# Setup of a gated cross-attention decoder: TensorE turns while the first transfer is under way, step sizes by halves, two activation tables loaded early

## What is computed

```python
x = x + tanh(g_xattn[0]) * selective_scan(ctx, layernorm(x), ...)      # this case's stretch
x = x + tanh(g_ffn[0])   * mixture_of_experts(layernorm(x), ...)       # 64 experts, 8 chosen, 64 slots each
x = x + tanh(g_xattn[1]) * attention(layernorm(x), ctx, ...)           # 16 heads, 8 key/value heads
x = x + tanh(g_ffn[1])   * ternary_weight_ffn(layernorm(x), ...)
```

```python
x  = einsum('bld,ed->bel', hidden_states, in_proj_w)            # 256 inner channels
x  = silu(causal_conv(x, conv_w, 4 taps) + conv_b)              # "u" below
dt_low, Bm, Cm = split(einsum('bdl,ed->bel', x, x_proj_w), [8, 24], axis=1)
dt = softplus(einsum('brl,dr->bdl', dt_low, dt_proj_w) + dt_proj_b)   # the step sizes
# for each token: state = state * exp(dt * A) + (dt * u) * B;  y = sum_n state * C, n = 0..15
y  = (y + D * x) * silu(z)
```

## Time and profile before

| | |
|---|---|
| Median of 3 runs | 565.86 us (564.44 to 566.52) |
| Profiled execution, own time | 564.71 us |
| its span in the trace | 563.0 us |
| TensorE busy | 483.5 us (86%) |
| VectorE busy | 456.3 us (81%) |
| ScalarE busy | 371.2 us (66%) |
| GpSimd busy | 283.3 us (50%) |
| bytes moved by DMA | 61.65 MB, 109 GB/s in the mean |

### The profile page before, as it was taken

The page is one execution under the profiler, slowest core; times in us unless marked ns, Lnnn a source line. Parts: engine busy times, 40 slices in busy tenths (PEclk is TensorE's granted clock), DMA queues, the critical chain, the costliest instruction groups (busy, mean ns, idle before and its releaser), DMA issues.

```text
span 563.0 us, 10640 instructions
## 1 busy us (share of the span) xinstructions
PE 483.5 (86%) x3374; PEld 396.7 (70%) x3374; DVE 456.3 (81%) x1213; ACT 371.2 (66%) x863; POOL 283.3 (50%) x254
## 2 busy tenths in 40 slices
PE   5955877778899799999899999989699898998835
PEld 3443555555689667767798999978699788996714
DVE  2879999999985678887568757987889879776887
ACT  2785766667346465878575766689466896788644
POOL 1118999989211755610586388434884343233111
PEclk9956999989999899999899999999999999999876
DMA  5976993322177799872421023200433000000000
GB/s 152 237 208 208 322 300 135 109 98 81 50 217 240 247 308 264 263 196 80 165 66 39 2 58 64 33 0 2 66 61 45 2 2 1 19 3 1 1 19 19
DMA packets 52477, 61.65 MB, mean 109 GB/s; under 512 B 6204, under 2 KB 42662, under 8 KB 52422
## 3 DMA queue, kind: packets, MB, share of 16 engines
q1 hardware_dynamic: 48582, 49.43, 30.1%
q0 software_dynamic: 3840, 11.54, 9.2%
HBM read 54.27 MB, written 6.69 MB: 108 GB/s over the span
## 4 chain that ended last, share of the span: by engine, by line
PE 37%; DVE 22%; issue 21%; POOL 9%; ACT 6%; DMA 3%; DVEq 0%; POOLq 0%; SPq 0%; ACTq 0%
PE ps L1661 6%; DVE hst L1913 5%; PE ps L1600 4%; PE ps L1601 4%; PE ps L1602 4%; PE ps L1650 3%; DVE hc L1925 3%; PE ps L1518 3%; POOL dbu L628 3%; POOL pn L711 2%; POOL G L695 2%; DMA ebuf<-state_rows 2%; PE ps L1554 2%; PE ps L1539 2%; POOL G L673 1%
## 5 line engine op out<-in xcount | busy, mean ns | idle before, releaser
L711 POOL TENSOR_TENSOR pn<-pr,pinv 128x512 f32<-128x512 f32 x64 | 67.6, 1058 | 88.2 <-DVE pinv L2326 87.8
L628 POOL TENSOR_TENSOR dbu<-du,brow 128x512 f32<-128x512 f32 x64 | 92.9, 1481 | 25.4 <-DVE du L1903 22.1
L1913 DVE TENSOR_TENSOR_SCAN hst<-ps,dbu 128x512 f32<-128x512 f32 x64 | 74.6, 1202 | 0.2 <-POOL dbu L628 0.2
L1057 ACT ACTIVATE pr<-ebuf,smin 128x256 f32<-128x256 f32 x128 | 63.8, 502 | 13.4 <-POOL pn L711 6.7
L854 ACT ACTIVATE ps<-dtv,amat 128x510 f32<-128x510 f32 x64 | 44.4, 694 | 36.0 <-DVE hst L1913 33.1
L1661 PE MATMUL ps<-pT,cS 128*128 128x256 f32 x256 | 66.5, 382 | 0.0
L673 POOL DMA_INDIRECT G<-token_rows,idx_x x32 | 37.8, 1180 | 43.3 <-DVE wkv L2050 20.8
L695 POOL DMA_INDIRECT G<-expert_out,idx_g x48 | 51.4, 1070 | 11.6 <-issue 10.5
L1600 PE MATMUL ps<-xnT,mqk 128*128 128x256 f32 x128 | 46.9, 366 | 6.7 <-DVE qT L2287 3.5
L2317 DVE CUSTOM_DVE_ANT_0 ebuf<-ps,mbias 128x256 f32<-128x256 f32 x128 | 49.0, 420 | 4.2 <-issue 3.9
L1302 PE MATMUL ps<-hc,ident 128*128 128x512 f32 x68 | 37.1, 636 | 16.1 <-DVE hc L1925 15.9
(11 more groups left out here) (381 smaller groups left out, 1438.3 us busy)
## 6 DMA issues: line engine op xcount, KB each, us to landing
brow<-state_rows SPq DMA_DIRECT2D x16, 512.0 KB, 5.0
wdn<-in_L_ffn_wd SPq DMA_DIRECT2D x12, 384.0 KB, 8.3
ebuf<-state_rows SPq DMA_DIRECT2D x17, 256.0 KB, 3.8
wgu<-in_L_ffn_wg SPq DMA_DIRECT2D x11, 384.0 KB, 6.0
wgu<-in_L_ffn_wu SPq DMA_DIRECT2D x11, 384.0 KB, 8.7
expert_out<-xn SPq DMA_DIRECT2D x11, 256.0 KB, 5.3
wq<-in_L_xattn_Wq SPq DMA_DIRECT2D x2, 1024.0 KB, 7.4
wo<-in_L_xattn_Wo SPq DMA_DIRECT2D x1, 2048.0 KB, 11.6
```

The source lines that it names most:

```text
L628: nc.gpsimd.tensor_tensor(dbu[:, j, :], du[:, j % 2, at:at + 512], brow[:, pair % BRING, j // 2, :], ALU.mult).then_inc(pool_dbu, 1)
L711: nc.gpsimd.tensor_tensor(pn[:, h % 2], pr[:, h % 2], pinv[:, h % 2, :].unsqueeze(2).to_broadcast([P, 2, L]), ALU.mult)\
L1057: last = A(pr[:, h % 2, tt, :], sneg[:, h % 2, tt, :], ACT.Exp, scale=-1.0, bias=smin[:, h % 2, tt:tt + 1], accum_out=psum_[:, h % 2, tt:t ...
L1913: V.tensor_tensor_scan(hst[:, j, :], bank(j % 2), dbu[:, j, :], 0.0, ALU.mult, ALU.add)\
```

## The change

1. TensorE, once the identity is there and before it waits for the context, turns the identity 16 times into bank 7. Nobody reads the result.
2. ScalarE applies Silu to a spare value after its first copies, and Exp to a spare value after the last Relu, so that the tables for these functions are loaded there.
3. Raw step sizes and all operations on them go by half: first tiles 0 and 1 of tokens 0 to 511, then of tokens 512 to 1023. Each operation has 512 columns instead of 1024, and there are twice as many. TensorE's loop over L1288 has the half outside and the tile inside. VectorE still makes both halves ahead of the first scan; the two small memsets of decay columns come between the halves.
4. Waits follow: GpSimd waits for du of half 0 at pair 0 and of half 1 at pair 8, ScalarE for all four dt at scan 32, SyncE before Wk and Wv for all four dt.

```diff
@@ SyncE
-            sp_.wait_ge(dt_ready, 2)
+            sp_.wait_ge(dt_ready, 4)
@@ GpSimd, drive(pair, j)
-                if pair == 0 and j < 2:
-                    pool.wait_ge(du_ready, j + 1)
+                if pair % (NS // 2) == 0 and j < 2:
+                    pool.wait_ge(du_ready, 4 * pair // NS + j + 1)
@@ ScalarE
             A(winT[:, 0], bank(5).rearrange("p (k e) -> p k e", k=NCONV), ACT.Copy).then_inc(winT_ready, 1)
+            act.wait_ge(consts_ready, 3)
+            chain.link(A(spare_table[:, 0:1], mhalf[:, 0:1], ACT.Silu))
...
-            for d in range(DT):
-                act.wait_ge(dtraw_done, 2 * d + 2)
-                chain.link(A(sp[2 * d][:], ps[:, 2 * d:2 * d + 2, :].rearrange("p a b -> p (a b)"), ACT.Abs,
-                             bias=dtb[:, d:d + 1]))
-                A(sp[2 * d + 1][:], sp[2 * d][:], ACT.Exp, scale=-1.0).then_inc(sp_exp, 1)
-            for d in range(DT):
-                act.wait_ge(sp_u, d + 1)
-                A(dtv[:, d], sp[2 * d][:], ACT.Ln).then_inc(sp_ln, 1)
-                A((rest, dtlow)[d][:], ps[:, 2 * d:2 * d + 2, :].rearrange("p a b -> p (a b)"), ACT.Relu,
-                  bias=dtb[:, d:d + 1]).then_inc(sp_relu, 1)
+            def at(hb):
+                return slice(512 * hb, 512 * hb + 512)
+
+            for hb in range(2):
+                for d in range(DT):
+                    act.wait_ge(dtraw_done, 2 * hb + d + 1)
+                    chain.link(A(sp[2 * d][:, at(hb)], bank(2 * d + hb), ACT.Abs, bias=dtb[:, d:d + 1]))
+                    A(sp[2 * d + 1][:, at(hb)], sp[2 * d][:, at(hb)], ACT.Exp, scale=-1.0).then_inc(sp_exp, 1)
+            for hb in range(2):
+                for d in range(DT):
+                    act.wait_ge(sp_u, 2 * hb + d + 1)
+                    A(dtv[:, d, at(hb)], sp[2 * d][:, at(hb)], ACT.Ln).then_inc(sp_ln, 1)
+                for d in range(DT):
+                    A((rest, dtlow)[d][:, at(hb)], bank(2 * d + hb), ACT.Relu, bias=dtb[:, d:d + 1]).then_inc(sp_relu, 1)
+            A(spare_table[:, 1:2], mhalf[:, 0:1], ACT.Exp)
...
+                if i == 32:
+                    act.wait_ge(dt_ready, 4)
@@ TensorE
+            def keep_busy(k, count):
+                for _ in range(count):
+                    pe.transpose(ps[:, k, 0:P], ident[:], ident[:])
+
             pe.wait_ge(consts_ready, 1)
+            keep_busy(7, 16)
             pe.wait_ge(d_ctx, 16)
...
-            for d in range(DT):
-                for hb in range(2):
-                    pe.wait_ge(dtlow_ready, hb + 1)
+            for hb in range(2):
+                pe.wait_ge(dtlow_ready, hb + 1)
+                for d in range(DT):
                     pe.matmul(bank(2 * d + hb), dtwT[32:32 + DTR, P * d:P * d + P],
@@ VectorE
-            for d in range(DT):
-                dve.wait_ge(sp_exp, d + 1)
-                V.tensor_scalar(sp[2 * d][:], sp[2 * d + 1][:], 1.0, None, ALU.add).then_inc(sp_u, 1)
...
-                V.tensor_tensor(du[:, d], dtv[:, d], u[:, d], ALU.mult).then_inc(du_ready, 1)
+            for hb in range(2):
+                for d in range(DT):
+                    dve.wait_ge(sp_exp, 2 * hb + d + 1)
+                    V.tensor_scalar(sp[2 * d][:, at(hb)], sp[2 * d + 1][:, at(hb)], 1.0, None, ALU.add).then_inc(sp_u, 1)
+                for d in range(DT):
+                    dve.wait_ge(sp_u, 2 * hb + d + 1)
+                    chain.step(V.scalar_tensor_tensor(sp[2 * d + 1][:, at(hb)], sp[2 * d][:, at(hb)], -1.0,
+                                                      sp[2 * d + 1][:, at(hb)], ALU.add, ALU.subtract))
+
+            def step_sizes(hb, d):
+                n = 2 * hb + d + 1
+                dve.wait_ge(sp_ln, n)
+                chain.link(V.tensor_tensor(dtv[:, d, at(hb)], dtv[:, d, at(hb)], sp[2 * d + 1][:, at(hb)], ALU.subtract))
+                dve.wait_ge(sp_relu, n)
+                V.tensor_tensor(dtv[:, d, at(hb)], dtv[:, d, at(hb)], (rest, dtlow)[d][:, at(hb)], ALU.add)\
+                    .then_inc(dt_ready, 1)
+                dve.wait_ge(u_ready, 4)
+                dve.wait_ge(dt_ready, n)
+                V.tensor_tensor(du[:, d, at(hb)], dtv[:, d, at(hb)], u[:, d, at(hb)], ALU.mult).then_inc(du_ready, 1)
+
             chain.wait()
             for d in range(DT):
+                step_sizes(0, d)
+            dve.wait_ge(sp_relu, 3)
+            for k in range(2):
+                V.memset(bank(k).rearrange("p (b l) -> p b l", b=2)[:, :, 0:1], 0.0).then_inc(a_ready, 1)
+            for d in range(DT):
+                step_sizes(1, d)
```

More of the change, by code:

```diff
@@ L88, in build_program @@
         mhalf = sb("mhalf", [P, 8])
+        spare_table = sb("spare_table", [P, 2])
         x = sb("x", [P, NT, H])
@@ L1325, in turn_back @@
                     done.then_inc(y_added, 1)
-            def keep_busy(k, count):
-                for _ in range(count):
-                    pe.transpose(ps[:, k, 0:P], ident[:], ident[:])
             def turn_out(hb, b):
@@ L1892, in _ @@
             chain.wait()
             for d in range(DT):
[L1894 to L1900, removed]
@@ L1901, in _ @@
-                dve.wait_ge(u_ready, 4)
-                dve.wait_ge(dt_ready, d + 1)
-                V.tensor_tensor(du[:, d], dtv[:, d], u[:, d], ALU.mult).then_inc(du_ready, 1)
+                step_sizes(0, d)
[4 more added lines that the diff above has]
+                step_sizes(1, d)
             def scan(pair, j):
```

## The result

The changed kernel takes 568.2 us in the median of 20 runs (565.93 to 570.81); the kernel before, run beside it, takes 564.61 (562.38 to 568.66). The ratio is 1.0059 with a 95% interval of 1.0043 to 1.0076: the change costs 3.3 us. The profiled execution of the changed kernel has an own time of 568.11 us and a span of 566.4, 3.4 us over both values of before.

A forecast was written before the change was run, and what follows sets the result against it. Taken as bound by the setup chain on TensorE, VectorE and ScalarE, whose shift reaches the end through the scan: pair 1 +2.1 us and rhythm +0.7 make +2.8 on a mean of 565.4, so 568.2 us; range 563.6 to 570.4.

The forecast's parts named there:

- four collisions: GpSimd's four pair 0 products fall between VectorE's half 1 steps from 39.0 us, costing 1.0 us each; first scan at 47.25.
- What bounds the kernel: Setup chain up to VectorE's last step-size product at 44.17 us; a shift of scan pair 1 passes to the end.
- Part 1: Sixteen TensorE turns before the context raise the clock by L1254: 1.1 us less 0.1 delay, 1.0 us gained; bounds 0 and 1.1.
- The rule weighed beside it: Skill's statement that transpose mode doesn't count as PE-busy the same way; by it the turns are worth 0, total 1.0 to 1.2 longer.
- rival A: The turns do not raise the clock; first Abs stays at 28.36, +3.8 us, 569.2; chance 0.18.
- Part 2: ScalarE's Silu and Exp table loads move into idle time or after the last Relu; worth 0.
- Part 3: Step sizes by halves: undisturbed they all stand at 43.25 us against 44.17 before; GpSimd's products then delay VectorE.
- B: VectorE leaves GpSimd no opening, or its products fall behind; one collision as before, +0.1 us, 565.5; chance 0.12.
- C: Short operations do not exclude each other; first scan 43.25, -1.9 to -0.9 us, 564.0; chance 0.10.
- D: Every part works as written and ready products spare VectorE scan waits; -2.9 us or more, below 562.9; chance 0.05.
- The rhythm: In the scan, GpSimd's full buffers make pairs 6.18 us instead of 5.82; bounds 0 and 1.4 us, taken 0.7.
- SyncE's wait: Before loading Wk and Wv, SyncE waits for the fourth dt until 46.5 instead of 42.85; worth 0, 3.7 us without cover.

The follow-up runs named there:

- tables_only: The kernel before with only the two early table loads (spare Silu and Exp) added; 564.59 us, ratio 0.9988.
- no_turns: The changed kernel without the sixteen early TensorE turns; 569.78 us, ratio 1.0070 against the kernel before.
- before_again: The kernel before with no edit, one more traced execution; 567.25 us.
- turns_only: The kernel before with only the sixteen early TensorE turns added; 565.04 us, ratio 0.9998.
- turns_relag: turns_only with GpSimd's first product held back at pairs 7 and 12; 565.40 us, ratio 1.0039 against the kernel before.
- hold_all: The changed kernel with GpSimd waiting at pair 0 for all four du; 566.31 us, ratio 1.0024 against the kernel before.
- defer: The changed kernel with VectorE's step sizes for half 1 moved behind scan pairs 0 and 1; 577.88 us, ratio 1.0278 against the kernel before.
- hold_two: The changed kernel with GpSimd making two products early at pair 0, then waiting for all four du; 565.25 us, ratio 1.0036 against the kernel before.
- turns_again: The same program as turns_only, measured once more; 565.10 us, ratio 1.0013 against the kernel before.

## Why the prediction was right, and where it was not

The forecast was 568.2 us, and the median is 568.2; the sum was +2.8, measured +3.3 by the ratio. The mechanism of the loss was right: four collisions, where and when they were forecast. The gain that was set against it, 1.0 us for the turns, did not come. That the total agrees to 0.1 us is luck: the base, 565.4 from four executions, was 0.8 above the 564.61 measured beside the changed kernel, and the sum was 0.5 below the measured change.

**What bounds the kernel.** Right for this stretch: the shift of pair 1 passed to the end of the scan (2.4 there, 2.9 at the last product with C) and to the end of the span (3.4).

**Part 1, the turns.** This is the term that was mis-sized: "The sum is 1.1 less the 0.1 of delay". The four products did run in 1.96 us, the statistics did start at 13.8 and the first Abs at 27.47 (forecast 27.36). But the comparison row was one execution with a late context. Over executions the delay of the real turns is 0.4 to 0.9 us, the clock is sometimes up without the turns (tables_only, no_turns), and where it is not an early context nearly makes up for it (before_again). Measured: 0.9998 and 1.0013 for the turns alone, in the mean +0.3 us with an error of about 0.8, and the -1.0 of the sum is outside that. The pair with the halves (1.0059 with the turns, 1.0070 without) gives -0.6 with an error of about 1.7, which decides nothing.

**The rule weighed beside it.** In turns_only the context's eight turns take 1.04 us, 0.13 each, where the sixteen before them took 0.22 each, and TensorE had done nothing but turns until then. In before_again, without the sixteen, the same eight take 1.94. When the rise comes differs: in the changed kernel the eight take 1.50, in turns_relag 1.91. But in all ten traces with the sixteen turns the level is up by L1254, in those without them in two of four. So turning did raise the clock in this kernel, and rival A, the low clock, did not come. The Trainium skill, TensorE: Matmul & The Clock Gate, Part 4, has it that turns don't count as busy in the same way; these traces speak against it. A's consequence for the time (turns worth nothing) came all the same, as far as the runs show because the context lands early and x late.

**Part 2, the tables.** Right: the Silu load lies at 9.89, in ScalarE's idle time, the Exp load ends at 39.62 (39.7 forecast), and tables_only measures no difference.

**Part 3, the halves.** Half 0's `du` stood at 39.27 (forecast 38.95), the B row landed at 39.04 (39.0). Four collisions, as forecast, cost 1.04, 0.95, 0.87 and 1.06 over 0.69, 3.9 in all (4.0 taken); the first scan started at 47.50 (47.25), pair 1 at 53.70 (53.4). hold_all shows the undisturbed case: 43.58, forecast 43.25. Rivals B and C, in which GpSimd finds no opening or short operations don't exclude each other, fall with the same rows, and D with the result. The Trainium skill, SBUF — State Buffer, Who interferes with whom, describes such a lock, held for a whole instruction, between a GpSimd instruction that reads SBUF and a VectorE operation with two SBUF inputs. The trace agrees with it at this size of 512 columns: 1.56 to 1.75 us with a GpSimd product in between (1.26 alone), 0.69 without.

**The rhythm.** Pair 1 came 6.20 after pair 0 (6.2). The lateness grew from 2.4 at pair 1 to 3.7 near 77 us, the +1.4 that was the upper bound, and the two waits of the kernel before then gave back 1.1. The 0.7 taken in the middle turned out as a net of +0.2 at the fifth product shown and +0.5 at the last: both bounds' mechanisms were at work one after the other. turns_relag shows the rhythm itself (2.92 against 3.10).

**SyncE's wait.** Right at nothing: it issued Wk 3.9 us later, and no reader noticed. defer shows what it costs when the cover is gone: VectorE idle for 5.78 us.

**The sum.** Turns about +0.3 where -1.0 was taken, halves about +3.2 where +3.8 was taken. Together +3.5, beside the measured +3.3 and the +2.8 of the forecast. The halves' size holds within its error of about 1 us, and the traces put it at 3.6; the turns' does not. Two side figures don't follow from the prediction's own terms: the upper edge "up to +4.9" (2.1 with collisions of 1.2, which add 0.8, and 1.4 for the rhythm make +4.3), and rival D's "below 562.9" (565.4 - 2.9 is 562.5). Neither touches the forecast.

## What to carry to other kernels

Cutting operations in half so that a neighbour engine may start sooner also lets it start among them. Before doing it, list what the neighbour will run beside the rest, and what the two exclude each other on; here each 512-column GpSimd product cost VectorE about 1 us, four times. Don't price a gain of under 1 us in the front of a kernel from one trace, since the landing of the first transfer alone moves by as much; trace the same program twice, and count from a landmark behind the scatter. Timings of several pairs of kernels that differ in the same way say more than one pair: here single pairs gave 2.8 and 5.2 us for the same edit. When a step is put off, follow every wait on it through the queue that holds other loads, as the 22.0 us of SyncE showed.

## What the runs showed of the hardware that I had not expected

- The same instructions start differently from one execution to the next: TensorE could start on the context at 4.77 to 4.98 us in three executions and at 5.62 in a fourth, and the first four products of TensorE took 3.75 us in two executions without the turns and 1.96 in two others with the same TensorE work up to there. The granted clock of the records reads 1.00 in both kinds, so that early in the span the durations tell the level and the record doesn't.
- After 2.0 us of idleness TensorE's granted clock fell to 0.50 in one execution (hold_two) and stayed at 1.00 in others with a gap as long (2.08 in turns_only, 2.14 in no_turns). What decides was not found.
- Where GpSimd has all four buffers full, a half pair of scans takes 3.09 us instead of 2.91, and the product with C takes 0.92 instead of 0.73, which is the whole difference. In turns_again the GpSimd product before it ends at 130.66, 0.38 us after the product with C is started (130.28); in turns_relag it ends at 131.54, 0.20 after (131.34). So a producer that is ahead can slow its consumer down.
